# Graph attention on one Trainium2 core: per-group sums by plain products with the identity in place of transposing ones

## What is computed

```
z = layernorm(x);  q, k, v = z @ Wq + bq, z @ Wk + bk, z @ Wv + bv
scores = sum_d(q[row] * k[col]) / 8 + edge_bias            # per edge and head
p = exp(scores - segment_max(scores, row)[row])
att = segment_sum(p / segment_sum(p)[row] * v[col], row) @ Wo + bo
x1 = x + att;  y = silu(layernorm(x1) @ W1 + b1) @ W2 + b2  # hidden width 1024
out = layernorm(x + x1 + y)
```

## Time and profile before

| | |
|---|---|
| median of 3 runs | 3471.95 us (lowest 3470.25) |
| profiled execution | 3467.36 us |
| its span (first to last instruction) | 3465.6 us |
| phase 2, first to last `sum_d` (L1474) | 1480.8 to 3399.3 us |
| PE, DVE, ACT, POOL busy over the span | 81%, 75%, 50%, 68% |
| granted clock of PE, mean | 0.874 |

### The profile page before, as it was taken

One profiled execution on the slowest core, in us unless ns is written; L12 is line 12 of the kernel. 1 busy time (PEld: TensorE's weight loads), 2 busy tenths in 40 slices (PEclk: granted clock), 3 DMA queues, 4 the chain that ended last, 5 costly groups with the idle time before them and its releaser, 6 DMA issues.

```text
span 3465.6 us, 82992 instructions
## 1 busy us (share of the span) xinstructions
PE 2801.8 (81%) x18957; PEld 2153.2 (62%) x18958; DVE 2586.1 (75%) x6243; ACT 1732.6 (50%) x6760; POOL 2363.3 (68%) x2599
## 2 busy tenths in 40 slices
PE   8666666666666666477999999999999999999997
PEld 7433333333333333266888888888888888787885
DVE  9877667766766776467787888888877777777774
ACT  0111111111111111157787888888877777787774
POOL 0477777777777777677777777776666666666661
PEclk9866776666667776689999999999999999999999
DMA  8222222222232222378798888888788888888770
GB/s 303 84 80 79 79 81 80 90 82 77 78 81 81 77 77 79 119 279 320 296 335 308 320 312 324 317 315 317 280 304 286 319 286 320 290 294 308 253 266 25
DMA packets 287972, 719.26 MB, mean 208 GB/s; under 512 B 89203, under 2 KB 105779, under 8 KB 287686
## 3 DMA queue, kind: packets, MB, share of 16 engines
q0 software_dynamic: 214080, 585.55, 47.8%
q1 hardware_dynamic: 73862, 133.41, 11.8%
HBM read 725.41 MB, written 72.97 MB: 230 GB/s over the span
## 4 chain that ended last, share of the span: by engine, by line
issue 30%; POOL 27%; PE 16%; DMA 10%; ACT 7%; POOLq 4%; DVE 3%; ACTq 2%; DVEq 0%; SPq 0%; PEld 0%; PEldq 0%
POOL records L413 19%; POOL region_a L537 8%; ACT region_c L740 6%; DMA records<-region_c,pos_i 6%; PE bank L1474 6%; PE wide L1533 2%; PE bank L1374 2%; PE wide L1545 2%; DMA region_c<-x_rows,row_x 2%; PE wide L1492 2%; PE bank L1517 1%; ACTq L740 1%; ACTq L778 1%; DVE region_c L978 1%; PE wide L1502 1%
## 5 line engine op out<-in xcount | busy, mean ns | idle before, releaser
L537 POOL DMA_INDIRECT region_a<-kv,cols x1176 | 1172.4, 997 | 428.1 <-issue 409.5
L413 POOL DMA_INDIRECT records<-region_c,pos_i x1024 | 1010.6, 987 | 444.6 <-issue 410.8
L740 ACT ACTIVATE region_c<-region_a,pr 128x64 f32 x4704 | 1171.1, 336 | 0.0
L1034 DVE TENSOR_TENSOR region_c<-region_a,bank 128x1024 f32<-128x1024 f32 x588 | 681.1, 1214 | 60.8 <-SPq L371 47.2
L1474 PE MATMUL bank<-ident,region_c 128*128 128x128 f32 x4704 | 595.9, 281 | 95.0 <-DVE region_c L1034 94.8
L1474 PEld LDWEIGHTS bank<-ident,region_c 128*128 128x128 f32 x4704 | 569.1, 195 | 125.7 <-issue 111.4
L1492 PE MATMUL wide<-ident,region_c 128*128 128x128 f32 x4704 | 576.5, 276 | 25.9 <-ACT region_c L740 14.0
L1492 PEld LDWEIGHTS wide<-ident,region_c 128*128 128x128 f32 x4704 | 523.4, 144 | 67.4 <-ACT region_c L740 67.4
L660 ACT COPY region_c<-region_a 128x64 f32 x128 | 32.5, 254 | 1062.5 <-DMA records<-region_c,pos_i 1062.5
L1432 PE MATMUL bank<-region_b,region_a 128*128 128x512 f32 x768 | 491.2, 798 | 0.0
L1432 PEld LDWEIGHTS bank<-region_b,region_a 128*128 128x128 f32 x768 | 189.7, 260 | 253.7 <-issue 253.7
(11 more groups left out here) (197 smaller groups left out, 3276.4 us busy)
## 6 DMA issues: line engine op xcount, KB each, us to landing
region_a<-srcT SPq DMA_DIRECT2D x128, 256.0 KB
region_a<-kv,cols POOLq DMA_INDIRECT x1176
region_a<-hiT SPq DMA_DIRECT2D x256, 64.0 KB
records<-region_c,pos_i POOLq DMA_INDIRECT x1024
x_rows<-region_c SPq DMA_DIRECT2D x32, 512.0 KB
kv<-region_a SPq DMA_DIRECT2D x32, 512.0 KB
records<-region_c SPq DMA_DIRECT2D x32, 480.0 KB, 15.0
region_a<-in_x_dram SPq DMA_DIRECT2D x32, 256.0 KB
```

Source lines behind the costliest of these rows:

```text
L413: pool.indirect_dma_start(records, bass.IndirectOffsetOnAxis(ap=pos_i[j % 2][:, s:s + 1], axis=0), rec_w[j % 2][:, s, :], None).then_inc(S ...
L537: pool.indirect_dma_start(KV[r][:, s, :], None, kv, bass.IndirectOffsetOnAxis(ap=cols[r][:, s:s + 1], axis=0), bounds_check=L - 1, oob_is_ ...
L740: last = act.activation(vw[:, s, of], v_part[:, s, C + hd * D:C + (hd + 1) * D], ACT.Copy, scale=pr[:, s + 1, hd:hd + 1])
L1034: last = dve.tensor_tensor(prods[:, of, :], kv_in[:, of, 0:C], q_ps[:, :].unsqueeze(1).broadcast_to([P, 2, C]), ALU.mult)
```

## The change

Both sums are made the other way around: the identity is the weights and the data moves, without `is_transpose`, so that nothing comes out turned.

- `sum_d`: 16 matmuls of 256 moving columns (4 parts x 64 pairs of slot and head; neighbours in this order lie 64 words apart in `prods`), 8 in each half. `take_scT`, `turn_scores`, `fold` and the PSUM tile `scT_ps` go. DVE adds the 4 parts with one reduce of PSUM (`gather_parts`, 256 words to 64) and a drain before `add`.
- `products`: the four instructions are cut by parts of the head rather than by slots: each takes 4 slots and, of every run of 16 words, 8. The first two need all slots landed.
- `sum_v`: 8 matmuls of 512 moving columns, straight onto `acc_ps`; `take_vT`, `turn_sum`, `vT_ps`, `vT_sb` and the semaphores of them go. `scale` and the final division wait for `SUMMED[3]`; `sum_v` of pair 0 waits for `acc_taken`. In PE's order `sum_d(1)` now follows the pieces of `up` or `down_side`, and `sum_v` follows it at once; at stage 1 its first matmul starts the sum afresh.
- `s_all` has three buffers (`KEPT`); POOL waits for `out_sent` before the next output's row numbers, and the wait for `xb_loaded` with the copy of `row_x` moves from the start of a tile to `tail_rows`, after its second group.

```diff
-    SH = SUB * HEADS
-    FOLD = P // SH
+    SH = GROUP * HEADS
+    RUN = D // FOLD
+    PART = RUN // 2
...
-        scT_ps, sc_ps = bank[0][:, 0:2 * P], bank[0][:, 2 * P:2 * P + 2 * SH]
-        vT_ps, acc_ps = bank[1], bank[7]
+        sc_ps = bank[0][:, 0:FOLD * SH]
+        acc_ps = bank[7]
...
+                with pool.If(t > 0):
+                    hold(S["xb_loaded"], pool.snap(n_x) * 16)
...
-            def take_scT():
-                act.wait_ge(S["scT_ready"], now)
-                act.wait_ge(S["sc_summed"], groups)
-                act.copy(scT_sb, scT_ps).then_inc(S["scT_sb_ready"], 1)
-            def take_vT():
-                act.wait_ge(SUMMED[3], now)
-                act.wait_ge(S["acc_ready"], groups)
-                act.copy(vT_sb, vT_ps[:, :]).then_inc(S["vT_sb_ready"], 1)
...
             def products():
                 kv_in = slots(at)
-                dve.wait_ge(S["scT_ready"], groups)
-                for pair in range(PAIRS):
-                    of = slice(2 * pair, 2 * pair + 2)
-                    dve.wait_ge(LANDED[pair], now)
-                    last = dve.tensor_tensor(prods[:, of, :], kv_in[:, of, 0:C],
-                                             q_ps[:, :].unsqueeze(1).broadcast_to([P, 2, C]), ALU.mult)
-                    if pair % 2:
-                        last.then_inc(PRODS[pair // 2], 1)
+                for a in range(2):
+                    for s in range(0, GROUP, SUB):
+                        of = slice(s, s + SUB)
+                        if a == 0:
+                            dve.wait_ge(LANDED[s // 2], now)
+                            dve.wait_ge(LANDED[s // 2 + 1], now)
+                        last = dve.tensor_tensor(piece(prods[:, of, :], a), piece(kv_in[:, of, 0:C], a),
+                                                 q_ps[:, :].rearrange("p (k i) -> p k i", i=RUN)[:, :, a * PART:(a + 1) * PART]
+                                                 .unsqueeze(1).broadcast_to([P, SUB, HEADS * FOLD, PART]), ALU.mult)
+                    last.then_inc(PRODS[a], 1)
...
+                def gather_parts():
+                    dve.wait_ge(S["sc_summed"], groups)
+                    dve.tensor_reduce(sc_in[:, :], sc_ps.rearrange("p (j k) -> p k j", j=FOLD), AX.X, ALU.add)
...
-            prod_cols = prods.rearrange("p s (h j i) -> p i (s h) j", h=HEADS, j=FOLD)
+            prod_cols = prods.rearrange("p s (h j i) -> p i j (s h)", h=HEADS, j=FOLD)
             def sum_d(a):
                 if a == 0:
-                    pe.wait_ge(S["scT_sb_ready"], groups)
                     pe.wait_ge(S["sc_ready"], groups)
                 pe.wait_ge(PRODS[a], now)
-                for i in range(D // FOLD):
-                    last = pe.matmul(scT_ps[:, a * P:(a + 1) * P], prod_cols[:, i, a * SH:(a + 1) * SH], ident[:, :],
-                                     start=i == 0, stop=i == D // FOLD - 1, is_transpose=True)
+                for i in range(a * PART, (a + 1) * PART):
+                    last = pe.matmul(sc_ps, ident[:, :], prod_cols[:, i], start=i == 0, stop=i == RUN - 1)
                 if a == 1:
-                    last.then_inc(S["scT_ready"], 1)
-            def turn_scores():
-                pe.wait_ge(S["scT_sb_ready"], now)
-                for a in range(2):
-                    last = pe.matmul(sc_ps[:, a * SH:(a + 1) * SH], scT_sb[:, a * P:(a + 1) * P], fold[:, :], start=True, stop=True)
-                last.then_inc(S["sc_summed"], 1)
-            def sum_v(pair):
+                    last.then_inc(S["sc_summed"], 1)
+            def sum_v(pair, first=False):
                 if pair == 0:
-                    pe.wait_ge(S["vT_sb_ready"], groups)
+                    pe.wait_ge(S["acc_taken"], now)
                 pe.wait_ge(V_READY[pair], ahead)
                 for s in (2 * pair, 2 * pair + 1):
-                    for c in range(KT):
-                        last = pe.matmul(vT_ps[:, c * P:(c + 1) * P], vw[:, s, c * P:(c + 1) * P], ident[:, :],
-                                         start=s == 0 and c == 0, stop=s == GROUP - 1, is_transpose=True,
-                                         skip_group_check=True)
+                    last = pe.matmul(acc_ps, ident[:, :], vw[:, s, :], start=first and s == 0, stop=s == GROUP - 1,
+                                     skip_group_check=True)
                 last.then_inc(SUMMED[pair], 1)
-            def turn_sum(first=False):
-                pe.wait_ge(S["vT_sb_ready"], groups)
-                pe.wait_ge(S["acc_taken"], groups)
-                for c in range(KT):
-                    last = pe.matmul(acc_ps[:, c * P:(c + 1) * P], vT_sb[:, c * P:(c + 1) * P], ident[:, :],
-                                     start=first and c == 0, stop=c == KT - 1, is_transpose=True, skip_group_check=True)
-                last.then_inc(S["acc_ready"], 1)
...
                 sum_d(0)
-                if stage < 2:
-                    with pe.If(t > 0):
-                        turn_sum()
-                else:
-                    turn_sum(stage == 2)
-                sum_d(1)
                 if 0 < stage < STAGES:
...
-                turn_scores()
+                sum_d(1)
...
```

More of the change, by code:

```diff
@@ L24 @@
 PAIRS = GROUP // 2
+FOLD = 4
 PEEL = 5
@@ L425, in _ @@
             pool.wait_ge(S["rows_ready"], 1)
-            names = "groups now ring side off page_left late pages since n_resets n_late n_row n_sent n_x count ahead left".split()
-            groups, now, ring, side, off, page_left, late, pages, since, n_resets, n_late, n_row, n_sent, n_x, count, ahead, left = (
+            names = "groups now ring side off page_left late pages since n_resets n_late n_row n_sent n_x count ahead left kept".split()
+            groups, now, ring, side, off, page_left, late, pages, since, n_resets, n_late, n_row, n_sent, n_x, count, ahead, left, kept = (
                 pool.alloc_register(f"pool_{name}") for name in names)
-            for r in (groups, ring, side, off, late, pages, since, n_resets, n_late, n_row, n_sent, n_x, ahead):
+            for r in (groups, ring, side, off, late, pages, since, n_resets, n_late, n_row, n_sent, n_x, ahead, kept):
                 pool.reg_mov(r, 0)
@@ L547, in tail_rows @@
                     hold(S["out_ready"], pool.snap(n_sent))
-                    with pool.If(pool.snap(side) > 0):
-                        send(1)
+                    with pool.If(pool.snap(kept) < 1):
+                        send(0)
+                        pool.reg_mov(kept, 1)
                     with pool.Else():
-                        send(0)
+                        with pool.If(pool.snap(kept) < 2):
+                            send(1)
+                            pool.reg_mov(kept, 2)
+                        with pool.Else():
+                            send(2)
+                            pool.reg_mov(kept, 0)
+                with pool.If(t > 0):
+                    hold(S["xb_loaded"], pool.snap(n_x) * 16)
+                    copy_rows(row_x[:, :], tile_row(bass.ds(pool.snap(nc.s_assert_within(t - 1, 0, NT - 2, skip_runtime_bounds_check_because="the If has t > 0")), 1))[:, 0:1])
                 pool.nop()
@@ L725, in exponents, with weigh @@
                 act.copy(sc[:, 0, :], m_run[:, :]).then_inc(S["max_kept"], 1)
-            def weigh(pair, reg, freed, t=None, first=False):
+            def weigh(pair, reg, freed):
                 v_part = region_a[:, bass.ds(act.snap(reg, min_val=0, max_val=(RING - 1) * HALF), HALF)].rearrange("p (s c) -> p s c", s=GROUP)
@@ L779, in body @@
                 exponents()
-                weigh(0, at, now, t, i is None)
+                weigh(0, at, now)
                 if i is None:
@@ L1089, in below @@
                                       ALU.subtract).then_inc(S["sc_ready"], 1)
-                return add, largest, below
+                return gather_parts, add, largest, below
             def together(*chains):
@@ L1101, in softmax @@
             def softmax(bias):
-                add, largest, below = softmax_steps(bias)
+                gather_parts, add, largest, below = softmax_steps(bias)
+                gather_parts()
+                dve.drain()
                 add()
@@ L1344, in _ @@
             middle(NT)
-            hold(S["out_sent"], 16 * (NT - 2))
+            hold(S["out_sent"], 16 * (NT - 3))
             residual(half(NT - 1))
@@ L1588, in body @@
                 else:
-                    sum_v(0)
+                    sum_v(0, stage == 1)
                     sum_v(1)
```

80 lines of the change are left out of this document (33 added, 47 removed).

## The result

The changed kernel takes 5147.4 us (median of 4), the kernel before 3472.2 us beside it: 1.483 times as long, 95% interval 1.480 to 1.486. It is slower by 1675 us, where 691 were forecast; the range ended at 4330. The profiled execution has a span of 5144.8 us. One of the four runs of the kernel before, 13541 us beside three of 3470 to 3472, is left out of the ratio.

What follows compares the result with a forecast made beforehand. PE's work was taken as the bound. The profiled 3467.4 us, plus 693 for the stretch (2613 us, 35 of them waiting, against 1920) and 2.4 for the tail, gave 4163 us; range 4110 to 4280, stretched to 4330.

Steps and rivals of the forecast that it cites:

- What bounds the kernel: Phase 2: PE's own work is the bound, with some 1 us of waiting a group from the turn by ACT.
- Two records for a plain product: PE matmuls: a plain float32 product runs as two records, a transposing one as one; the sums grow 5.68 us a group.
- The stride of the moving columns: New `sum_d`, neighbouring columns 256 bytes apart: no cost taken, though 50 us (54 rounded upward) or 588 us were considered.
- The near row: Old `sum_d`'s weight load at 64-byte steps: at most 0.88 ns a column, so 225 ns against 215 for 256 columns.
- The far row: L1374, 64 columns at 16-byte steps, weights and moving: 1.33 ns a column, so 340 ns for 256 columns.
- rival (a): New `sum_d`: the stride of the moving columns bites in full, 588 us more, 4750 us; chance 11%.
- The rest of the sum: Whole kernel without stride cost: stretch 2613 us including 35 us of waits, tail +2.4 us, total 4163 us.
- DVE hidden, ACT hidden, POOL hidden: Beside PE's 17.7 us a group: DVE's 11 us hides, ACT has no more to do, POOL's queue has 5 us slack.
- The buffers and row numbers "worth nothing on PE's path": DVE's and POOL's waits removed, 59.7 and 57.6 us: worth nothing, as those engines aren't the bound.
- (b): PE's sums: a product with the identity runs as one record, giving 3308 us; chance 3%.
- (c): DVE becomes a second bound, slower products and reduce, 1.5 us a group, 220 us, 4380 us; chance 5%.
- The waits that go: PE's waits for ACT's copied scores (63 us) and for ACT's pair 3 (73 us) both go.

Runs made afterwards that it cites:

- v_only: The kernel before with the V part of the change alone (`sum_v` by plain products, `turn_sum` and the copy gone); 3783.1 us, 1.088 to 1.091.
- s_only: The kernel before with the scores part alone, four neighbouring words as columns, and three residual buffers, V as before; 3741.6 us, 1.076 to 1.079.
- plain_turned: The kernel before with `is_transpose` taken off `sum_d` alone, products still the weights; 4927.6 us, 1.420.
- step16: The changed kernel with `sum_d`'s moving columns 16 bytes apart, a jump every 4 columns; 5146.3 us.
- run4: The changed kernel with `sum_d`'s moving columns 4 bytes apart, a jump every 4 columns; 4129.6 us.
- flat: The changed kernel with DVE writing products in PE's order, so `sum_d`'s moving columns are contiguous, 4 bytes throughout; 4137.6 us.
- kept: The kernel before with only the three residual buffers, the `out_sent` wait and the moved `row_x` copy of the change; 3436.8 us, 0.990.

## Why the prediction was wrong

- **What bounds the kernel**: right. PE's work bounds it before, and after it is 99.7% busy; v_only and s_only cost what PE's added distances cost, less its waits, to 12 us.
- **Two records for a plain product**: right in count (4704 and 2352, and 9408 in plain_turned), and `sum_v` at 6.87 us for 6.88.
- **The stride of the moving columns**: this step failed. "I take no cost" and the bounds 0 and 588 us stood against 1025 us. The near row, `sum_d`'s weight load at 64-byte steps within 112.5 ns, was near in tile, type and step, and far in what counts: it was of a transposing matmul. plain_turned shows that a plain one with the same load takes 215 ns a record. The far row, L1374 with 1.33 ns a column, was bfloat16 with 64 columns, and even it lay under the 1.69 ns of a float32 record, so rival (a) at 4750 had the right mechanism and too small a price. The rule of the Trainium skill (Advanced Engine Details and Errata, section Memory Cachelines), which the prediction quoted, was the better guide: a different line for each access is what step16 shows to cost double.
- **The rest of the sum**: with that stride away, run4 takes 4129.6 us for a forecast of 4163. That is inside the range of 4110 to 4280. From first to last `sum_d` it has 2568 us (1487.0 to 4054.6) where 2613 were forecast. Of these 45 us, 24 are waits: 35 were kept and 11 are there. The other 21 are not traced to a term. The way to the first `sum_d` is 6 us longer than before, which no term had, and the time after the last one starts is 7 us longer, where 2.4 were forecast. So the 4130 are near the forecast partly because small errors of both signs meet. The least cost of the stride, put at 50 us, is 47 by its own figures (32 x 0.010 x 147).
- **DVE hidden, ACT hidden, POOL hidden**: right; even flat's products of 1.93 us are, but for 8 us.
- **The buffers and row numbers "worth nothing on PE's path"**: wrong for the kernel before by 33 us (kept); DVE's wait of up to 4.4 us was long enough to make products late for PE. Beside the longer PE work of the changed kernel there is no such wait left, so this didn't move the forecast.
- **Rivals**: (b), one record a product, is excluded by the counts. (c), DVE as a second bound, didn't occur: its products stayed at 1.21 us, its reduce at 0.42. The direction, slower, was right; the size was not.
- **The waits that go**: right. The waits for the copied scores and for pair 3, put at 63 and 73 us, were 69.5 and 67.4 in the kernel before, and neither is among PE's waits after.

## What to carry to other kernels

Exchanging data and identity in a float32 sum doesn't save columns: 32 x 128 in transposing matmuls are as many as 8 x 512 plain ones, and the plain ones ran twice. Look at the records per source matmul before counting on a layout that "comes out right". Where a plain float32 matmul reads scattered operands, arrange the order so that at least two neighbours come from the same 16 bytes: here it was a choice of which 16 of 64 words go into one matmul, which cost nothing and saved 1018 us. And a row is near another case only if the instruction's mode is the same too.

## What was not expected of the hardware

- A plain float32 matmul took 0.84 ns a moving column with steps of 4 or 8 bytes and 1.69 ns with 16, 64 or 256 bytes (216 and 218 against 432, 431 and 433 ns for 256 columns), with no value in between; a step of 12 bytes wasn't tried.
- The same doubling on the weight side: 128 columns at 64-byte steps took 215 ns a record in plain matmuls and 112.5 ns in transposing ones; contiguous ones took 112 ns in plain matmuls.
- DVE's products of 1024 words, 1.21 us when written in rows or in runs of 8 words, took 1.93 us when written with steps of 1024 bytes.
